# A windowed-attention network on one core: the output projection from rounded parts, the value projection through another PSUM bank, and the norm's floor in another instruction

## What is computed

```python
def attn_layer(x, Wqkv, qs, ksc, Wo):           # 16 heads of 64, windows of 32 tokens
    q, k, v = split(x @ Wqkv, 3)
    q = l2norm(q) * qs                          # t / max(norm(t), 1e-12), per head
    k = l2norm(k) * ksc
    q = q * cos * scale + rotate_half(q) * sin * scale
    k = k * cos / scale + rotate_half(k) * sin / scale
    out = local_attention(q, k, v)              # each window sees itself and the one before it
    return out @ Wo                             # 1024 -> 128
def ffn_layer(x, g, bln, W1, b1, W2, b2):       # layer norm, then a * gelu(gate)
    ...
```

## Time and profile before

| | |
|---|---|
| median of 3 runs | 4177.26 us (4172.37 to 4178.75) |
| the profiled execution | 4182.92 us, its span 4181.1 us |
| busy share of the span | PE 93%, DVE 79%, ACT 74%, POOL 62% |
| mean granted clock of TensorE | 0.986 of full speed |
| one step of stage 2, without layer-norm work and without a stall | 7.34 us |

### The profile page before, as it was taken

How to read it: one execution, slowest core, us unless ns; L and a number is a source line. 1 busy time by engine, 2 the same in 40 slices (tenths; PEclk the granted TensorE clock), 3 DMA queues, 4 the chain that set the end, 5 groups by cost and what they waited for, 6 DMA issues and landing times.

```text
span 4181.1 us, 190344 instructions
## 1 busy us (share of the span) xinstructions
PE 3900.5 (93%) x78816; PEld 3039.7 (73%) x78816; DVE 3305.5 (79%) x5294; ACT 3091.6 (74%) x10376; POOL 2581.2 (62%) x2583
## 2 busy tenths in 40 slices
PE   6888885999998999989999989999899999899998
PEld 3555554888866888848888668888488887588884
DVE  6778874988866888938888668989489886698894
ACT  5877785888865888838888658888488886588883
POOL 4667765766645676627666456766377664566660
PEclk9999998999999999999999999999999999999999
DMA  1000001111111111111111111111111111111110
GB/s 35 2 2 2 2 2 53 47 45 45 46 56 38 45 47 45 44 50 44 49 44 46 58 36 47 44 49 42 53 44 47 47 44 61 35 45 46 47 43 26
DMA packets 100195, 167.40 MB, mean 40 GB/s; under 512 B 26224, under 2 KB 33648, under 8 KB 99056
## 3 DMA queue, kind: packets, MB, share of 16 engines
q1 hardware_dynamic: 99312, 154.89, 12.6%
HBM read 26.13 MB, written 2.10 MB: 7 GB/s over the span
## 4 chain that ended last, share of the span: by engine, by line
PE 69%; issue 9%; POOL 3%; DVE 1%; ACT 0%; DMA 0%; SPq 0%; POOLq 0%; DVEq 0%; ACTq 0%
PE s_bank L1177 13%; PE s_bank L1246 10%; PE s_bank L1259 9%; PE s_bank L1198 8%; PE s_bank L1157 5%; PE s_proj L1222 4%; PE s_proj L1223 4%; PE s_proj L1224 4%; PE s_bank L1209 2%; PE s_bank L1210 2%; PE s_bank L1211 2%; PE s_bank L1167 2%; PE s_bank L1140 1%; POOL s_rotated L802 1%; PE s_bank L1289 1%
## 5 line engine op out<-in xcount | busy, mean ns | idle before, releaser
L802 POOL TENSOR_TENSOR s_rotated<-s_rotated,s_by_sin 128x512 f32<-128x512 f32 x768 | 983.8, 1302 | 227.3 <-DVE s_by_sin L1087 225.2
L811 POOL TENSOR_TENSOR s_probs<-s_probs,s_rden 128x256 f32<-128x256 f32 x768 | 479.7, 641 | 729.8 <-DVE s_rden L1027 729.3
L901 ACT ACTIVATE s_probs<-s_bank,s_neg_max 128x64 f32<-128x64 f32 x3072 | 908.0, 310 | 5.7 <-DVE s_neg_max L1020 5.6
L783 DVE TENSOR_TENSOR s_qk<-s_rotated,s_inv_norm 128x1024 f32<-128x1024 f32 x384 | 743.8, 1937 | 11.5
L1082 DVE TENSOR_TENSOR s_rotated<-s_proj,s_cos 128x1024 f32<-128x1024 f32 x384 | 469.6, 1223 | 241.5 <-ACT s_sq L935 240.9
L901 ACT ACTIVATION_READ_ACCUMULATOR s_probs<-s_bank,s_neg_max 128x1 f32 x3072 | 636.1, 207 | 0.0
L891 ACT ACTIVATE s_probs_t<-s_bank 64x512 f32<-64x512 f32 x384 | 226.8, 591 | 524.8 <-PE s_bank L1157 524.8
L1177 PE MATMUL s_bank<-s_qk 32*32 32x64 f32 x49152 | 581.4, 223 | 26.3 <-issue 25.9
L1177 PEld LDWEIGHTS s_bank<-s_qk 32*32 32x32 f32 x49152 | 510.9, 103 | 115.4 <-issue 114.6
L213 POOL TENSOR_TENSOR s_probs<-s_probs,s_rden 128x384 f32<-128x384 f32 (+3 forms) x512 | 406.4, 802 | 206.1 <-DVE s_rden L406 202.2
L824 POOL TENSOR_TENSOR s_sq<-s_sq 128x512 f32<-128x512 f32 x384 | 490.2, 1277 | 65.5 <-ACT s_sq L935 59.8
(11 more groups left out here) (118 smaller groups left out, 8156.2 us busy)
## 6 DMA issues: line engine op xcount, KB each, us to landing
s_v<-s_v SPq DMA_DIRECT2D x384, 192.0 KB, 2.5
s_v<-s_v SPq DMA_DIRECT2D x384, 64.0 KB, 2.4
s_qk<-f_wqk SPq DMA_DIRECT2D x6, 1024.0 KB, 6.4
s_xs_raw<-u SPq DMA_DIRECT2D x48, 128.0 KB
s_xf<-u SPq DMA_DIRECT2D x48, 128.0 KB, 2.3
s_xs_raw<-u SPq DMA_DIRECT2D x48, 127.8 KB
s_xf<-u SPq DMA_DIRECT2D x48, 127.8 KB, 2.6
s_qk<-f_wv SPq DMA_DIRECT2D x6, 512.0 KB, 6.8
```

Of the source, the lines that this page charges most:

```text
L783: return nc.vector.tensor_tensor(qk[:, quad % 2, :, :, at:at + TOKS], rotated[:, par, :, :, :], by, ALU.mult)
L802: nc.gpsimd.tensor_tensor(rotated[:, par, :, half, :], rotated[:, par, :, half, :], by_sin[:, :, 1 - half, :], (ALU.subtract, ALU.add)[half])\
L811: nc.gpsimd.tensor_tensor(part, part, by, ALU.mult).then_inc(S["probs_done"], 1)
L901: last = nc.scalar.activation(probs[:, par, h, b, :], score_bank[h][:, b * KEYS:(b + 1) * KEYS], ACT.Exp, scale=-1.0, bias=neg_max[:, par, ...
```

## The change

1. **Output projection.** The weights `wo` join `w_high` and `w_rest` (4096 columns in place of 3072). ScalarE's copy of y goes to `y_high` in fp32r, and VectorE gets a new instruction per step, `y_rest` = `y_bank` - `y_high` for piece n-5, placed behind the first reciprocal. TensorE runs three fp32r matmuls for each of the two pairs, 6 in a step, and waits for `y_rest` as well as `y_done` ahead of them.
2. **Banks and order.** The value projection goes into `tr_bank`, behind the copies of the transposes, and `vy_bank`, now `y_bank`, holds only y. TensorE's order becomes: scores, transposes (now also after `v_done` of the step before), sums of squares, queries and keys, values, output projection of n-5, product with the values of n-4. ScalarE copies the values behind the squares.
3. **The norm's floor.** VectorE's L1064 is gone; ScalarE takes the logarithm straight out of `ss_bank` with a small bias, ahead of the copy of y. `write_qk` becomes two instructions of 512 columns, each (inverse norm min 1e12) times rotated.

```diff
@@ write_qk (VectorE)
-            by = inv_norm[:, par, :, :].unsqueeze(2).to_broadcast([P, 2, 2, TOKS])
-            return nc.vector.tensor_tensor(qk[:, quad % 2, :, :, at:at + TOKS], rotated[:, par, :, :, :], by, ALU.mult)
+            for i in range(2):
+                by = inv_norm[:, par, i, :].unsqueeze(1).to_broadcast([P, 2, TOKS])
+                last = nc.vector.scalar_tensor_tensor(qk[:, quad % 2, i, :, at:at + TOKS], by, NORM_CUT,
+                                                      rotated[:, par, i, :, :], ALU.min, ALU.mult)
+            return last
@@ ScalarE
-                if full:
-                    act.wait_ge(S["v_mm"], n + 1)
-                    nc.scalar.activation(v[:, p // TILES, 2 * (p % TILES), :], vy_bank[:, :], ACT.Copy)
...
                     nc.scalar.activation(sq[:, :, :, :], proj_ps[:, :, :, :], ACT.Square)
+                    act.wait_ge(S["v_mm"], n + 1)
+                    nc.scalar.activation(v[:, p // TILES, 2 * (p % TILES), :], tr_bank[:, :], ACT.Copy)
+                if live(s, p, LAG_MIX, first):
+                    act.wait_ge(S["ss_done"], m + 1)
+                    nc.scalar.activation(inv_norm[...], ss_bank[:, :], ACT.Ln, scale=LN_SCALE, bias=log_floor[:, 0:1])
...
-                    nc.scalar.activation(y[:, place(p, LAG_VALUE)[2], :, :],
+                    nc.scalar.activation(y_high[:, place(p, LAG_VALUE)[2], :, :],
...
-                    act.wait_ge(S["guard_done"], m + 1)
-                    nc.scalar.activation(inv_norm[:, par, :, :], inv_norm[:, par, :, :], ACT.Ln, scale=LN_SCALE)
@@ VectorE
-                    dve.wait_ge(S["ss_done"], m + 1)
-                    nc.vector.tensor_scalar(inv_norm[...], ss_bank[:, :], NORM_FLOOR, None, ALU.max)
                 if score:
                     inverse_sum(0)
+                if live(s, p, LAG_WO, first):
+                    m, par = n - LAG_WO, place(p, LAG_WO)[2]
+                    dve.wait_ge(S["y_done"], m + 1)
+                    nc.vector.tensor_tensor(y_rest[:, par, :, :], y_bank[...], y_high[...].bitcast(F32), ALU.subtract)
@@ TensorE, behind the projection of queries and keys
+                    pe.wait_ge(S["pt_first"], n - LAG_VALUE + 1)
+                    pe.wait_ge(S["pt_second"], n - LAG_VALUE + 1)
+                    pe.wait_ge(S["v_done"], n)
...
+                    nc.tensor.matmul(tr_bank[:, :], xs_rest[:, s % 2, toks], wv[0][:, cols], start=False, stop=True)
+                if live(s, p, LAG_WO, first):
+                    pe.wait_ge(S["y_done"], m + 1)
+                    pe.wait_ge(S["y_rest"], m + 1)
+                    for pair in range(2):
+                        nc.tensor.matmul(into, w[0], y_high[:, par, pair, :], ...)
+                        nc.tensor.matmul(into, w[0], y_rest[:, par, pair, :], ...)
+                        nc.tensor.matmul(into, w[1], y_high[:, par, pair, :], ...)
                 if live(s, p, LAG_VALUE, first):
+                    mixed = y_bank[:, :].rearrange("p (x t a e q) -> p x t a e q", x=2, t=NT, a=2, e=2)
...
-                if live(s, p, LAG_WO, first):
-                    for pair in range(2):
-                        nc.tensor.matmul(wo_bank[...], wo[:, 2 * quad + pair, :], y[:, par, pair, :], ...)
```

More of the change, by code:

```diff
@@ L647, in build_stage2 @@
         probs_t = sb("s2_probs_t", [P, 2, NT, HPG, 2, WIN])
-        y = sb("s2_y", [P, 2, 2, TOKS])
-        w_raw = qk[:, :, :, :, WIN:].rearrange("p a i c t -> p (a i c) t")[:, 0:(QUADS * 4 * P + INNER) // SEQ, :]
+        y_high = sb("s2_y_high", [P, 2, 2, TOKS], F32R)
+        y_rest = sb("s2_y_rest", [P, 2, 2, TOKS], F32R)
+        w_raw = qk[:, :, :, :, WIN:].rearrange("p a i c t -> p (a i c) t")
         in_rows = lambda w: w.rearrange("p (r t) -> p r t", t=SEQ)
@@ L1226, in step @@
                     last.then_inc(S["proj_done"], 1)
+                if full:
+                    if live(s, p, LAG_VALUE, first):
+                        pe.wait_ge(S["pt_first"], n - LAG_VALUE + 1)
+                        pe.wait_ge(S["pt_second"], n - LAG_VALUE + 1)
+                    if not (first and p == 0):
+                        pe.wait_ge(S["v_done"], n)
+                    toks, cols = slice(p % TILES * P, (p % TILES + 1) * P), slice(p // TILES * (INNER // 2), (p // TILES + 1) * (INNER // 2))
+                    nc.tensor.matmul(tr_bank[:, :], xs_high[:, s % 2, toks], wv[0][:, cols], start=True, stop=False)
+                    nc.tensor.matmul(tr_bank[:, :], xs_high[:, s % 2, toks], wv[1][:, cols], start=False, stop=False)
+                    nc.tensor.matmul(tr_bank[:, :], xs_rest[:, s % 2, toks], wv[0][:, cols], start=False, stop=True)\
+                      .then_inc(S["v_mm"], 1)
+                if live(s, p, LAG_WO, first):
+                    m = n - LAG_WO
+                    quad, half, par = place(p, LAG_WO)
+                    pe.wait_ge(S["y_done"], m + 1)
+                    pe.wait_ge(S["y_rest"], m + 1)
+                    if p == LAG_WO and not first:
+                        pe.wait_ge(S["attn_res"], l * NSEQ + s)
+                    for pair in range(2):
+                        into, w = wo_bank[:, half * TOKS:(half + 1) * TOKS], [part[:, 2 * quad + pair, :] for part in wo]
+                        nc.tensor.matmul(into, w[0], y_high[:, par, pair, :], start=(p == LAG_WO and pair == 0),
+                                         stop=False, skip_group_check=True)
+                        nc.tensor.matmul(into, w[0], y_rest[:, par, pair, :], start=False, stop=False, skip_group_check=True)
+                        last = nc.tensor.matmul(into, w[1], y_high[:, par, pair, :], start=False,
+                                                stop=(quad == QUADS - 1 and pair == 1), skip_group_check=True)
+                    last.then_inc(S["wo_done"], 1)
                 if live(s, p, LAG_VALUE, first):
@@ L1251, in step @@
                     last.then_inc(S["pv_done"], 1)
-                if live(s, p, LAG_WO, first):
-                    m = n - LAG_WO
-                    quad, half, par = place(p, LAG_WO)
-                    pe.wait_ge(S["y_done"], m + 1)
-                    if p == LAG_WO and not first:
-                        pe.wait_ge(S["attn_res"], l * NSEQ + s)
-                    for pair in range(2):
-                        last = nc.tensor.matmul(wo_bank[:, half * TOKS:(half + 1) * TOKS], wo[:, 2 * quad + pair, :],
-                                                y[:, par, pair, :], start=(p == LAG_WO and pair == 0),
-                                                stop=(quad == QUADS - 1 and pair == 1), skip_group_check=True)
-                    last.then_inc(S["wo_done"], 1)
                 if s == NSEQ and p == 0:
```

72 lines of the change are left out of this document (31 added, 41 removed).

## The result

The changed kernel takes 4518.68 us (median of 4 runs, 4503.84 to 4531.90), the one before 4174.82 us beside it: a ratio of 1.0823, 95% interval 1.0787 to 1.0859. It is slower, as forecast, but by 344 us in place of 156, and outside the range. The profiled execution's span is 4514.4 us, 333 above that of before. TensorE's mean granted clock is 0.981 against 0.986: a difference of 0.5%, about 20 us by an estimate from the span, so the clock is not the main cause.

The account below looks back on a forecast made before the run. TensorE bounds the kernel at 7.34 us a step, rising to 7.66. Terms 123 - 10 + 46 + 8 - 17 + 6 give 156 over the profiled 4182.9, so 4339; the runs' median is 5.7 lower: 4333 us, range 4235 to 4400.

Parts of the forecast that it names:

- where the wait arises: Output projection: TensorE gets `y_rest` at T + 3.84, arriving at T + 3.57; T is the start of a step's first transpose.
- the two paths and the collision: `y_rest` inside one step: at least 7.44 us; over two steps, with `write_qk` waiting for GpSimd's rotation: 7.66 each.
- the term for pauses: TensorE's pauses, 67 us before: those falling where it would wait anyway vanish, a quarter taken, -17 us.
- The saving of the output projection: On TensorE, six matmuls take 0.80 us where four took 0.97, saving 0.17 a step; otherwise unchanged, a step would be 7.17.
- L815's turn: At position 3, GpSimd's L815 runs between the halves of `write_qk`: 1.3 later, 0.2 given back, 46 us in 42 sequences.
- the statistics: Layer-norm steps: statistics remain at 0.85 us, 0.2 absorbed twice a sequence; with a later delay, net 8 us.
- 123 - 10 + 46 + 8: Longer steps 123 us, first five steps per layer without output projection -10, L815 at position 3 46, layer-norm steps 8.
- much slower, the halves each held up by a rotation: Rival, chance 0.04: each half of `write_qk` waits for one rotation, 1.2 us more in one step of four, 4450.
- The signs named for the profile: TensorE idle 0.3 to 0.6 us for `y_rest` in nearly every step, about 90% busy, L815 between halves, longer ScalarE waits.
- The alternation of 7.45 and 7.9: Sign in the profile: steps alternate about 7.45 and 7.9 us, mean near 7.66 without layer-norm work.

Follow-up runs that it names:

- the run with `y_rest` early: The changed kernel with VectorE making `y_rest` ahead of `write_qk`, TensorE's list unchanged: 4194.75 us, ratio to before 1.0035.
- The run with the wait alone: The kernel before, with TensorE also waiting for the same step's L1064 ahead of the product with the values: 4419.52 us, ratio 1.0577.
- the run with values last: The changed kernel with the value projection's three long matmuls moved behind the output projection: 4632.55 us, ratio 1.1096.
- The run with one write: The changed kernel with `write_qk` as one plain product of 1024 columns, without the cut at 1e12: 4480.73 us, ratio 1.0727.

## Why the prediction was right or wrong

**Right: where the wait arises, and when TensorE goes on.** The forecast had the output projection start at T + 4.06 on average (7.66 less the 3.60 behind it). In the 270 full steps of the changed kernel without a layer-norm statistic it starts at T + 4.07. The order of VectorE's list as the cause is shown by the run with `y_rest` early (4518.7 to 4194.8), where it starts at T + 3.48 at the median, and by the wait put into the kernel before, which alone made it 240 us slower.

**Right: the two paths and the collision.** 7.49 to 7.53 is the shortest step (7.44 forecast). `write_qk` takes 1.29 quiet (1.40 forecast) and ends 1.15 after a rotation (1.25 forecast).

**Wrong: the term for pauses, "I take a quarter: -17".** This is the step that failed. The forecast took the pauses as fixed events, some of which a wait would hide. They are not: the wait makes more of them. From mask to transposes the forecast kept 1.72 in its steps; measured is 2.26 on average. The pauses' sum in the scores rose from about 57 us (0.15 x 378) to about 181 (0.48 x 378), +124 in place of -17. That is 141 of the 177 us that were missing in the span. The run with the wait alone shows the direction (pauses of 60.9 us in place of 25.9), the run with values last shows that what stands behind the wait takes most of them away, and the run with `y_rest` early has them back at about the old level with TensorE's list unchanged.

**The saving of the output projection: right without the wait, less behind it.** The forecast had 0.80 for the six matmuls where the four took 0.97. In the run with `y_rest` early they take 0.79 on average to the product with the values, and a clean step there is 7.18 (7.17 forecast). Behind a wait they take 0.87: the first product's way to the second is 0.20 in the timeline, not 0.12. That is 0.07 in a step, about 25 us. The forecast also had TensorE arrive at T + 3.57, a start read in the old order; in the new order it arrives at T + 3.48, so the wait is 0.59 long in the steps without a statistic and not 0.49. The scores without a pause take 1.78, not 1.72, 23 us; why is open.

**Wrong by size: L815's turn.** It was put at 46 us, with 1.3 read from the earlier trace rows, where the rows give 1.21 (2135.75 less 2134.54). The run with one write measured 38 for it and the shorter write together, 21 of them at position 3.

**Missed: the statistics.** The forecast had them "remain at 0.85". They take 0.96 each in the changed kernel, against 0.86 before, and the second waits for the logarithm: from the product with the values to it are 1.60 us at position 6, where other steps have 1.09. The forecast looked at who reads the sums' bank only for ordinary steps. With `y_rest` late, taking this wait away was worth 8 us, not clear of the noise; with it early, 59.

**The account.** Span, after less before: 333. Of these 307 lie in the 354 full steps. Between the transposes and the mask it is 117 (154 since the last two blocks start later, 38 back for the shorter output projection), and 34 more for the statistics and the wait ahead of them; from mask to transposes it is 156, of which some 21 is the slower clean step and 135 pauses (124 over all 378, since in the draining steps they fell). The other 26 us lie at the layers' edges and elsewhere and are not attributed. Without its pauses and edges the forecast had 167 for these steps (123 - 10 + 46 + 8); measured without the pauses are 172. So its sum was right for the wait, by terms that partly offset each other, and the miss is the pauses. The rival "much slower, the halves each held up by a rotation" gave a time near the measured one (4450), but not its cause: halves held apart are seen at position 3, and there by L826.

**The signs named for the profile.** TensorE's 88% (90% named), the idle time ahead of the output projection put down to `y_rest`, L815 (now L826) between the halves and ScalarE's longer wait for the transposes (664.9 us in place of 524.8) are there. The alternation of 7.45 and 7.9 is not: of the 270 steps without a statistic 98 take less than 7.7, only 15 lie between 7.8 and 8.1, and 110 take 8.55 or more, by the pauses.

## What to carry to other kernels

When one engine is the bound and never waits, a new instruction that it awaits in the same step belongs at the head of the list that makes it, as early as its own inputs allow: here the place of one 0.7 us instruction was worth 324 us of 4519. Count a wait of TensorE ahead of many small matmuls at more than its length; here three long matmuls between the two took most of the added pauses away. And when an instruction moves to another engine, look up every reader and writer of its bank, also those that come once in eight steps.

## What was not expected of the hardware

- A wait of TensorE changes how often it pauses for instructions afterwards: 41 pauses and 25.9 us in the scores before, 157 and 122.7 us with a wait some 2 us ahead of them, 39 and 34.8 us with the same instruction list and no such wait. In all of these the scores go on some 2.4 to 2.5 us (median) after the start of a packet of the instruction queue.
- Two matmul kinds at the same width: float32 128 x 256 took 0.97 for 4 instructions with its change-over, fp32r 0.79 for 6, and 0.87 behind a wait. Three rounded products are a little cheaper than one float32 product, worth about 1% here once nothing waits for their inputs.
- GpSimd takes its turn at SBUF between two VectorE instructions that follow each other without a gap: at position 3 the second ended 2.34 us after the rotation and not 1.15.
